# Two-layer relational graph convolution on one core: reciprocals of counts kept in fp32 and loaded to all partitions by transfers

## The reference

```python
def _rgcn_layer(x, src, dst, edge_type, w_rel, root, bias):      # N = 12500, E = 200000, C = 128, 10 relations
    seg = dst * NUM_REL + edge_type
    sums = segment_sum(x[src], seg, N * NUM_REL)
    cnt = segment_sum(ones, seg, N * NUM_REL)
    mean = (sums / maximum(cnt, 1.0)[:, None]).reshape(N, NUM_REL, -1)
    return einsum('nrd,rdo->no', mean, w_rel) + x @ root + bias
edge_type = argmax(edge_attr_42[:, 16:26], axis=1)
h = relu(_rgcn_layer(x, ..., w_rel1, root1, b1))
out = layernorm(x + _rgcn_layer(h, ..., w_rel2, root2, b2))
```

## Time and profile before

| | |
|---|---|
| median of 3 runs | 3963.51 us (3960.76 to 3968.31) |
| profiled execution | 3968.87 us |
| its span, first to last instruction | 3967.2 us |
| POOL busy | 2988.3 us (75%) |
| PE busy | 2677.0 us (67%) |
| DVE busy | 1872.6 us (47%) |
| ACT busy | 375.5 us (9%) |
| DMA, mean over the span | 74 GB/s |

### The profile page before, as it was taken

How to read it: one execution, slowest core, us unless ns; L and a number is a source line. 1 busy time by engine, 2 the same in 40 slices (tenths; PEclk the granted TensorE clock), 3 DMA queues, 4 the chain that set the end, 5 groups by cost and what they waited for, 6 DMA issues and landing times.

```text
span 3967.2 us, 31733 instructions
## 1 busy us (share of the span) xinstructions
PE 2677.0 (67%) x10165; PEld 1801.4 (45%) x10166; DVE 1872.6 (47%) x2588; ACT 375.5 (9%) x399; POOL 2988.3 (75%) x3139
## 2 busy tenths in 40 slices
PE   4776777767777676777766666666665666666666
PEld 3444444444444444444454444444444444444444
DVE  6545545455554554545544343443434444343444
ACT  1010100101001010010100101010010100101000
POOL 7777777777777777777777777777777777777775
PEclk7887878788888887878888878787887887878788
DMA  4222232322323223232222222222222222222222
GB/s 132 77 84 86 78 94 78 94 74 78 95 78 94 74 78 94 78 89 66 81 67 60 66 62 63 62 65 62 62 63 65 63 62 62 65 62 63 62 63 58
DMA packets 151575, 293.69 MB, mean 74 GB/s; under 512 B 61620, under 2 KB 82504, under 8 KB 147959
## 3 DMA queue, kind: packets, MB, share of 16 engines
q0 software_dynamic: 100032, 205.07, 18.2%
q1 hardware_dynamic: 46630, 87.29, 6.7%
q10 hardware_dynamic: 4867, 0.79, 0.1%
HBM read 264.68 MB, written 28.25 MB: 74 GB/s over the span
## 4 chain that ended last, share of the span: by engine, by line
POOL 72%; issue 24%; PE 3%; POOLq 0%; DVE 0%; DMA 0%; ACT 0%; DVEq 0%
POOL rows L1400 72%; PE ps_agg L1820 1%; PE ps_agg L1817 1%; PE ps_out L1900 1%; PE ps_bc L1842 0%; POOLq L1436 0%; DMA rows<-in_x_dram,idx_s 0%; PE ps_out L1895 0%; DVE mean L2253 0%; DMA rows<-table,idx_s 0%; POOLq L1343 0%; POOLq L1430 0%; PE ps_bc L1854 0%; POOL mean L1396 0%; PE ps_out L1908 0%
## 5 line engine op out<-in xcount | busy, mean ns | idle before, releaser
L1400 POOL DMA_INDIRECT rows<-table,idx_s x1563 | 1484.2, 950 | 480.4 <-issue 480.4
L1400 POOL DMA_INDIRECT rows<-in_x_dram,idx_s x1507 | 1442.6, 957 | 459.3 <-issue 459.3
L1817 PE MATMUL ps_agg<-S_first,rows 128*128 128x390 f32 x1564 | 900.1, 666 | 1163.1 <-issue 743.5
L1820 PE MATMUL ps_agg<-S,rows 128*128 128x160 f32 (+2 forms) x4692 | 1244.5, 407 | 0.0
L2209 DVE TENSOR_TENSOR ring<-ps_agg,ring 128x429 f32 (+1 forms) x782 | 457.3, 585 | 1402.7 <-PE ps_agg L1820 696.8
L1820 PEld LDWEIGHTS ps_agg<-S,rows 128*128 128x128 f32 x4692 | 954.4, 243 | 351.2 <-issue 237.4
L1817 PEld LDWEIGHTS ps_agg<-S_first,rows 128*128 128x128 f32 x1564 | 339.6, 245 | 1404.1 <-issue 1049.1
L2195 DVE TENSOR_TENSOR S<-ps_iota,comb_b 128x1200 f32<-128x1200 f32 x392 | 547.6, 1397 | 0.0
L2253 DVE TENSOR_TENSOR mean<-ps_bc,ring 128x896 f32<-128x896 f32 (+2 forms) x284 | 300.7, 1061 | 502.8 <-PE ps_bc L1842 498.5
L1900 PE MATMUL ps_out<-mean,wall 128*128 128x448 f32 (+1 forms) x1120 | 499.8, 573 | 0.0
L1900 PEld LDWEIGHTS ps_out<-mean,wall 128*128 128x128 f32 x1120 | 225.1, 209 | 150.4 <-issue 141.0
(11 more groups left out here) (163 smaller groups left out, 811.8 us busy)
## 6 DMA issues: line engine op xcount, KB each, us to landing
attr<-in_edge_attr_dram SPq DMA_DIRECT2D x27, 1176.0 KB, 8.0
rows<-table,idx_s POOLq DMA_INDIRECT x1563, 2.5
rows<-in_x_dram,idx_s POOLq DMA_INDIRECT x1507, 2.5
x_in<-in_x_dram SPq DMA_DIRECT2D x54, 224.0 KB, 2.6
table<-h_s SPq DMA_DIRECT2D x54, 224.0 KB, 2.3
table<-outT SPq DMA_DIRECT2D x27, 224.0 KB, 3.6
xt_s<-table SPq DMA_DIRECT2D x27, 224.0 KB, 3.5
out_dram<-h_s SPq DMA_DIRECT2D x27, 224.0 KB
```

Of the source, the lines that this page charges most:

```text
L1400: pool.indirect_dma_start(out=rows[:, o, j, :], out_offset=None, in_=(x, table)[l][:, :], in_offset=bass.IndirectOffsetOnAxis(ap=at, axis= ...
L1817: ins = t_.matmul(sums, lhsT=rows[:, o, jj, :], rhs=S_first[:, PLACE[o], h, :, :], start=True, stop=False)
L1820: ins = t_.matmul(sums[:, :, lo:lo + w], lhsT=rows[:, o, jj, :], rhs=S[:, PLACE[o], h, j - 1, :].rearrange("p (r n) -> p r n", n=WN)[:, :, ...
```

## The change

The reciprocals are no longer split, stored as bf16 and spread by TensorE. In layer 0 `reciprocals` stops after the fp32 reciprocal (L2231 and L2234 stay, L2236 to L2243 go) for all halves but the last; SyncE stores that fp32 tile, waits until it has landed, and issues five loads, each of which puts two relations' reciprocals on all 128 partitions straight into `mean` (`load_counts`). Layer 1 makes the same loads, each once the transform that read those planes of `mean` is done (`types_done`). `scale` then multiplies `mean` with `ring`, both in SBUF, in place. The last half of layer 0 keeps the split and the spreads (`scale_spread`). `ps_bc`, now free, takes the edge types and the turned-back rows. `TYPES` and `MEANS` name other octs, and SyncE's transfers of a half stand in another order: the edge attributes are loaded, and the types turned, behind the counts and the rows, and rows of half `b-2` are saved where those of `b-1` were.

```diff
@@ SyncE
                 def save_counts(b, made):
                     sp.wait_ge(cnt_ready, made)
                     hold(b)
-                    sp.dma_start(rc_d[:, bass.ds(b * (HN // 2), nodes_of(b) // 2)],
-                                 rc_b[:, 0:nodes_of(b)].bitcast(F32)).then_inc(cnt_saved, 16)
+                    n = nodes_of(b)
+                    sp.dma_start(rc_d[bass.ds(b * (R * HN), R * HN)].rearrange("(r n) -> r n", n=HN)[:, 0:n],
+                                 rc_f[1][:, 0:n]).then_inc(cnt_saved, 16)
+
+                def load_counts(b, used):
+
+                    n = nodes_of(b)
+                    for k in range(5):
+                        if used is not None:
+                            sp.wait_ge(types_done[k] if k < 4 else out_ready, used)
+                            hold(b)
+                        sp.dma_start(mean[:, 2 * k:2 * k + 2, 0:n],
+                                     rc_d[bass.ds(b * (R * HN) + 2 * k * HN, 2 * HN)]
+                                     .rearrange("(a r n) -> a r n", a=1, n=HN)[:, :, 0:n].to_broadcast([P, 2, n])
+                                     ).then_inc(rc_in[k], 16)
...
+                    if not is_(b, 0):
+                        save_counts(b - 1, before)
+                        if not last:
+                            sp.wait_ge(cnt_saved, before * 16 if isinstance(b, int) else sp.snap(before * 16))
+                            load_counts(b - 1, None if is_(b, 1) else prev)
+                    if not (isinstance(b, int) and b < 2):
+                        save_part(b - 2, 0, HN, prev, h_s)
...
-                    sp.wait_ge(bc_ready[4], past)
-                    hold(b)
-                    sp.dma_start(rc_b[:, 0:n].bitcast(F32), rc_d[:, bass.ds(b * (HN // 2), n // 2)]
-                                 ).then_inc(cnt_in, 16)
...
+                    load_counts(b, past)
@@ TensorE: the table of spreads goes but for the last half of layer 0
-                SPREADS = {(1, 0): 0, (2, 0): 1, (2, 1): 2, (3, 1): 3, (4, 0): 4}
...
+                                if last and l == 0 and (o, h) in END_SPREADS:
+                                    spread(END_SPREADS[o, h], past)
@@ VectorE
-                    v_.reciprocal(f1, f0).then_inc(rc_step[1], 1)
+                    ins = v_.reciprocal(f1, f0)
+                    if split is None:
+                        ins.then_inc(cnt_ready, 1)
+                        return
...
+                def scale(b, par, lo, n, k, landed):
+
+                    dve.wait_ge(rc_in[k], landed)
+                    hold(b)
+                    here = mean[:, 2 * k:2 * k + 2, lo:lo + n]
+                    v_.tensor_tensor(here, here, ring[:, 2 * k:2 * k + 2, par * HN + lo:par * HN + lo + n], ALU.mult
+                                     ).then_inc(scaled[k], 1)
...
-                MEANS = {1: 0, 2: 1, 4: 4}, {2: 2, 3: 3}
+                MEANS = ({3: (2,), 4: (4,)}, {2: (0, 1), 3: (3,)}), ({}, {0: (0,), 1: (1, 2), 2: (3,), 3: (4,)})
```

More of the change, by code:

```diff
@@ L1530, in _ @@
                         nth, times = sp.snap(with_it + 1), sp.snap(with_it * 16 + 16)
+                    if not is_(b, 0):
+                        sp.wait_ge(xt_turned, before)
+                        hold(b)
+                    load_x(b, EARLY if last else HN)
+                    if last:
+                        load_x_end()
+                    prev = before - 1 if isinstance(b, int) else sp.snap(before - 1)
+                    if not is_(b, 0):
+                        save_counts(b - 1, before)
[4 more added lines that the diff above has]
+                        save_part(b - 2, 0, HN, prev, h_s)
+                    if last:
+                        sp.wait_ge(attr_used, HALVES)
+                        for o in range(2):
+                            load_late_src(o)
                     if not (isinstance(b, int) and b >= HALVES - 2):
@@ L1538, in _ @@
                         turn_typ(b + 1, nth, times)
-                    if not is_(b, 0):
-                        sp.wait_ge(xt_turned, before)
-                        hold(b)
[L1542 to L1550, removed]
+                save_part(END - 1, 0, HN, PARTS - 2, h_s)
                 save_part(*EARLY_PART, PARTS - 1, h_early)
@@ L1978, in _ @@
                                 aggregate(l, b, par, o, h)
-                                spreads = END_SPREADS if last else SPREADS
-                                if some and (o, h) in spreads:
-                                    spread(l, spreads[o, h], past, times)
-                                types = END_TYPES if last else TYPES
+                                if last and l == 0 and (o, h) in END_SPREADS:
+                                    spread(END_SPREADS[o, h], past)
+                                types = END_TYPES if last else TYPES[l]
@@ new lines, in _ @@
+                                    transform(l, 0, HN, types[o, h], past)
+                                if some and (o, h) == ((3, 1) if last else BACK[l]):
+                                    if l == 0 and last:
+                                        turn_back(0, HN, past)
+                                    else:
+                                        if not is_(b, 1):
+                                            if l == 0:
+                                                pe.wait_ge(h_ready, prev)
+                                            else:
@@ L2223, in fold, with reciprocals @@
                     dve.wait_ge(fold_done, before)
[L2225 to L2227 removed]
+                def reciprocals(par, lo, n, made, last_made, saved, split=None):
+                    f0, f1 = (f[:, lo:lo + n] for f in rc_f)
                     if last_made is not None:
@@ L2255, in scale, with centre @@
                                      ).then_inc(scaled[k], 1)
-                def centre(b, n, nth, last, made, landed, z=z_s, st=stat, x_rows=x_in, bank=ps_out):
+                def centre(b, n, nth, last, made, landed, z=z_s, st=stat, x_rows=x_in, bank=ps_back):
                     z, x_rows = blocks(z, n), blocks(x_rows, n)
@@ L2361, in _ @@
                                     make_S(1 - par, k, (agg_ready[4 + k], with_it))
-                            ahead_of, behind = END_MEANS if last else MEANS
-                            if some and o in ahead_of:
-                                scale(b, 1 - par, 0, HN, ahead_of[o], None if l == 0 and is_(b, 1) else prev, past)
+                            ahead_of, behind = END_MEANS if last else MEANS[l]
+                            for k in ahead_of.get(o, ()) if some else ():
+                                if l == 0 and last:
+                                    scale_spread(0, 0, HN, k, prev, 1)
+                                else:
+                                    scale(b, 1 - par, 0, HN, k, landed_rc)
                             if o == 5 and not (l == 0 and is_(b, 0)) and not (l == 1 and last):
```

146 lines of the change are left out of this document (76 added, 70 removed).

## The result

| | before | after |
|---|---|---|
| median | 3965.91 us (4 runs, 3960.76 to 3968.73) | 4014.59 us (4 runs, 4008.37 to 4018.58) |
| ratio | | 1.0123, 95% interval 1.0104 to 1.0142 |
| profiled execution, its span | 3968.87, 3967.2 us | 4012.17, 4010.5 us |
| POOL busy | 2988.3 us | 3034.0 us |
| PE busy | 2677.0 us | 2599.9 us |

The changed kernel is slower by 48.7 us, 1.2%. PE and DVE each do nearly 80 us less, and it costs time all the same.

What follows compares the result with a forecast made beforehand. POOL's queue of 3126 gathers was taken to bound the kernel. Scales +90, early five +1 and the dropped split -12 summed to +79 on 3963.5, giving 4042 us, range 4005 to 4095.

Steps and rivals of the forecast that it cites:

- The mechanism: A DVE instruction with both inputs in SBUF, running over a gather's start on POOL, makes that gather late.
- item 1: The 265 scales of 128x896, now with two SBUF inputs, make gathers late: 81 to 99 us, taken as +90.
- item 3: Five scales of 384 elements in a row, in the early part of layer 1's last half: +1 us.
- Even phases: Scales begin at any point of POOL's 1.25 us step alike: 0.346 us mean lateness each, 81 us for 53 halves.
- The factor 1.1: Raise on the scales' 81 us towards +90, after layer 1's small instructions showed 8.7 us where the form gave 7.1.
- Item 2: A waiting gather gets its turn between two back-to-back DVE instructions, as seen with three casts in the setup.
- the rival of a kept hold: DVE keeps its hold over back-to-back instructions, so pairs delay gathers by 1.30 us on average: 4091 us, chance 0.12.
- Item 4: Dropping the split, the five instructions behind the reciprocal in layer 0, removes late gathers: -12 us.
- Item 5: TensorE's spreads and the scales' 498.5 us wait for them go, but lie off the chain: worth nothing.
- Item 6: Five loads of 448 KB per half replace one of 65, some 124 MB more; DVE waits little: 0 us.
- Item 7: Start, change of layers and tail stay as they were: 0, give or take 3 us.
- phases locked: DVE's work follows the gathers' rows, so phases repeat: 3998 us with half the scales clear, 4085 with two thirds late; chance 0.15.

Runs made afterwards that it cites:

- e4: Changed kernel with one idle copy from PSUM ahead of scale 3 of each full half in layer 0: 4623.9 us, ratio 0.9931.
- e1: Changed kernel, full-half scales taking their first input from PSUM instead of the loaded mean, all loads kept: 4629.6 us, ratio 0.9948.
- e9: Same edit to the changed kernel as e1, measured again: 4638.5 us, ratio 0.9942.
- e11: Same edit to the changed kernel as e1, measured a third time: 4635.9 us, ratio 0.9939.
- e2: Kernel before, full-half scales reading their first input from SBUF instead of PSUM, spreads still made, nothing loaded: 4669.2 us, ratio 1.0030.
- e10: Same edit to the kernel before as e2, measured again: 4679.1 us, ratio 1.0026.
- e3: Kernel before without the split of the reciprocals in layer 0, for all halves but the last: 4648.6 us, ratio 0.9985.
- e5: Kernel before with reciprocals kept in fp32 and spread by fp32 matmuls on TensorE, no split: 3986.95 us, ratio 1.0053.
- e6: Kernel before with e5's fp32 spreads plus small operands of types, centring and normalisation moved to PSUM: 3974.33 us, ratio 1.0017.
- e8: Kernel before with e7's operands, fp32 spreads for halves 0 to 25, split and bf16 spreads for the last two: 4710.8 us, ratio 1.0089.
- e12: Same kernel as e8, measured where before takes 3968 us: 3945.67 us, ratio 0.9943.
- e7: Kernel before, split and bf16 spreads kept, only small operands of types, centring and normalisation moved to PSUM: 4664.45 us, ratio 1.0000.

## Why the prediction was right, and where a term was off

The 4014.6 us lie in the range of 4005 to 4095, near its lower end and 27 us under the 4042 that was forecast. It held them because it was 90 us wide, around a change of 49. The mechanism is the one that was forecast; its size was +79 and came out as +43 in the spans (+48.7 in the medians), and both errors, of item 1 and of the missing term below, go the same way.

- **The bound** held: POOL's queue is the chain, no new wait, the median gather 0.944 us. Budget and span agree within 0.1 us.
- **The mechanism** held, and with it the form: late by (end of the DVE instruction - start of the gather - 0.12), in 79 of 81 cases, and in 147 of 148 in the trace of e4. In the three exceptions the gather began within 0.02 us of the scale and was first, which the prediction had allowed for with its 0.04. e1, e9 and e11 take it away with the operand alone, e2 and e10 bring it with the operand alone.
- **Item 1, +90, measured 67, with item 3's early five 69.** The duration was right (1.084 us for 1.09), the chance of a strike was not. The step that failed is "if such an instruction begins at any point of POOL's 1.25 us step alike". Layer 0: singles 12.5, pairs 13.5; layer 1: 27.4 and 13.6. Even phases were near for the 52 pairs (0.346 + 0.14 each would give 25, found 27.1) and for layer 1's 83 singles (83 x 0.346 = 29, found 27.4); the failure is the 78 singles of layer 0 (27 by even phases, found 12.5). The factor 1.1, taken from a test on layer 1's small instructions, had no ground for the scales; it is 9 of the 23 us by which the term was too high.
- **A term that was missing, -10.** The types' two products in layer 0 and the normalisation and its like in layer 1 made 7.2 and 8.7 us of lateness before. After, what the scales don't explain is 2.8 and 3.0 us, with the same instructions still there. Their phases come behind those of the scales. That they were moved into the clear part is worked out from the remainder, not shown by a run.
- **Item 2, slipping in between,** held for these products too (the pair of 264.64), so the rival of a kept hold is out: by its form that gather would have been 1.52 late. (That rival's terms, 124 x 1.1 + 1 - 12 on 3963.5, give 4089 and not 4091.)
- **Item 3, the early five:** +1 forecast, 1.7 found, in one gather of 2.64 us.
- **Item 4, -12:** about 13 by the gathers, 11.8 by e3.
- **Item 5, spreads worth nothing:** right here; e5 and e6 show it would be wrong in the last half of either layer, and e8 that a lengthened spread costs time where POOL's queue does not end last.
- **Item 6, transfers 0:** 4.1 us to landing for 3.0 forecast, attributes 10.6 instead of 8.0, 120 MB more for 124; no scale waited for one.
- **Item 7, 0 give or take 3:** -2.3.
- Sum: 69 - 10 - 13 - 2 = +44, where the spans differ by 43.3, for +79. The rival "phases locked" had been given 0.15 with "half in the clear part, 3998"; what came is between it and the forecast, 4015, and its mechanism is the one at work in layer 0. The two are one case: some starts are locked and some not.
- **The rule.** The Trainium skill, page "SBUF — State Buffer", section "Who interferes with whom", infers that descriptor generation is spared by `tensor_tensor`. The measurement decides otherwise for these indirect gathers, where both inputs of the product are in SBUF: of the 81 single scales in after's trace that ran over a gather's start, 79 made it late by the form, while of before's 187 such scales, with one input in PSUM, none did.

## What to carry to other kernels

Where POOL's gathers are the chain, look at DVE's instructions by where their operands lie, not by their length: a 1.1 us product with one input in PSUM cost the gathers nothing, with two in SBUF it cost 0.2 to 0.3 us on average (layer 0 and layer 1 of after, e2). A second SBUF input is not the only thing to look for: in before's trace the split's three casts, from one SBUF tile to another, made 17 of the 19 gathers that began under them late, by 2.9 us in all, while 60 gathers began under the 2.9 us reciprocals of the same 10 partitions and none was late by the form. Such a cost depends on the phases, that is on how long after a gather's start the product begins. Read the phases in the trace before you take a mean: in layer 0 of after, delays set the rhythm anew and the phases bunched. And work that is free in the middle of a pipeline can be paid at its ends: keep the fast form for the last tiles, as e12 does.

## What was not expected of the hardware

**The same kernel, 3966 and 4654 us.** In three sessions before took 4654 to 4665 us. It does not follow the chip's number: number 13 gave 4664 in one session (e7 to e10) and 3968 in another (e12). Waits of POOL and one of PE in e1, and the granted clock by slices of the span, of before and then of e1:

```profile
POOL rows L1404 <- issue: 924.9, 2972, 2.2
POOL rows L1404 <- remote: 622.2, 144, 7.0
POOL rows L1404 <- DMA table<-attr: 45.9, 1, 45.9
...
PE ps_agg L1841 <- issue: 454.3, 340, 3.3
```

```profile
PEclk7887878788888887878888878787887887878788
```

```profile
PEclk6667777767777777777777776777777777776777
```

The gathers take 0.944 us there as elsewhere, and DVE's instructions what they take elsewhere. POOL waits 622 us, 144 times, for something that the trace does not name, and 46 at the change of layers; the granted clock averages 0.72 to 0.76 instead of 0.79 to 0.83. Late packets of the gathered rows are not the cause. The last of a gather's 32 packets ended 1.20 us (median) behind the gather in e1, and 1.19 in before; when the landing was signalled, e1's trace does not tell. But VectorE began to add a bank of sums 69 us (median) after the last gather that the bank needs, where before took 10.5, and 56 gathers, after which POOL comes back to a buffer, take 70. So POOL's waits there are most likely those for a buffer's sums (`agg_ready`), though no view names them. In e1 TensorE also has 340 pauses, 454 us, ahead of the matmuls of L1841, where the program has no wait; before has none there. What makes these pauses, and whether the clock has a part in it, stays open. What it does to an edit is plain: collisions cost little (15 us of time in e2 for 74 in its gathers, nothing visible in e4), and work on PE and DVE starts to count. The changed structure with its collisions (e4) is faster there by 0.7%, while e12's kernel, 0.6% faster where POOL's queue ends last, is 0.9% slower.

**The start alone decides.** A DVE instruction with both inputs in SBUF that ends 0.04 us into a gather costs nothing (after's scale of 1058.80 and gather of 1059.84); one that ends 1.04 in costs 0.92 (gather of 976.38). One that begins 0.05 or 0.21 us behind a gather's start costs it nothing either, however long it runs beside it (the gathers of 1056.10 and 1058.59, both 0.94 us).
